# A graph kernel whose grid of source blocks becomes a grid of pairs and eights, with two banks for the sums

## The chip, the cores and the metric

One Trainium2 chip, one of its cores. Times are device microseconds of one execution; a kernel is timed in several runs and the median is given. PE is TensorE, DVE VectorE, ACT ScalarE, POOL GpSimd, SP the queue that issues plain DMAs.

## The reference, cut to what matters

A graph network of 6250 nodes, 206250 edges sorted by destination, 64 features, four layers. In each layer an edge's message is made from its source's features and its own, and a softmax over the edges of a destination, feature by feature, weighs the messages:

```
msg = relu(h[src] + e) + 1e-7
ex = exp(t * msg - segment_max(t * msg, dst))
agg = segment_sum(msg * ex / segment_sum(ex, dst), dst)
out = h + agg
z = relu(layernorm(out @ w1 + b1)) @ w2 + b2      # then h = h + z, and a layernorm
```

`e = edge_attr @ enc_edge_w + enc_edge_b` is the same in all layers. At the start stands a node encoder, at the end a layernorm, a relu and the addition of x.

## The kernel before, in words

Destinations are sorted into 49 blocks of 128, the ones with the most overflow first. Each destination has a row of slots in DRAM (`ecell`), 64 features each, that holds its edges' encoded attributes. The first G slots are a grid: a slot for a group of source blocks. In a slot lies the first edge of this destination whose source is in the group; the nodes of the graph lie in 49 source blocks, of which the first 25 have a slot each and the other 24 share one in pairs, G = 37. Edges that find their slot taken go into overflow slots, V of them in a block (`OVER`, 36 to 6, 613 in sum), S = G + V.

`prepare` runs once. DVE finds for each edge whether an earlier edge of its destination has its cell (`dup`), counts the overflow with a scan (L456), and makes the target row of each edge. POOL scatters the encoded edges to these rows, 128 by an indirect DMA (`encoder`, L289), the first quarter here. Before that 98 DMAs on SP clear `ecell` (L364). DVE goes on with the node encoder (L554 to L582) and with counting rows (L534), for which POOL fetches rows (L526).

`lay` runs once. POOL scatters the other three quarters. Beside it `block` makes, for each destination block, a one-hot table for each source block (`ohd`): DVE reads from the slots which source lies in which slot (`hit`, `pick`, `code`, L798 to L807); PE spreads that number over the partitions (L822, a product with the identity), four slots in a bank; ACT casts it to bf16 (L830); DVE compares it with the partition's number (L837, for a pair twice, L842). SP writes the table of a block, 1568 KB (L847). ACT has the casts and the encoder's copies (L281) in one queue.

`layer` runs four times, three in a loop ("mid") and once more ("last"). For each destination block: SP loads its tables (L922) into one of two buffers; POOL gathers the overflow sources, one indirect DMA a slot (L929), and loads the block's slots from `ecell` (L914). PE (`passes`, L943) multiplies each one-hot table with the source block's features, kept as three bf16 parts, three products a table, eight slots to a bank of PSUM, and for a pair both blocks' into one slot. DVE adds the bank to the slots (`add`, L960) and the gathered rows to the overflow slots (`over`, L970), takes the maximum by halving (`most`, L981, L986), subtracts it (`sub`, L1002); ACT takes the exponent (L1008); DVE multiplies (`mul`, L1016). PE sums over the slots with the identity, four slots of weight and product by a matmul (L1026), and `fold` (L1036) adds the four. After every second block `node_unit` does the layernorms and the two linear maps on DVE, PE and ACT (L1055 to L1160), its steps woven between the operations of the next blocks.

The order is written out in the code and each engine takes its instructions in that order. In block d DVE does: `add` of d (with `passes` of d + 1 on PE, each bank free once it is added), `over`, `most`, `sub` of d, `fold` of d - 1, `mul` of d. PE does: `passes` of d + 1, the node step's products, the sums of d.

## Time and profile before

| | us |
|---|---|
| median of 3 runs | 8189.16 (8177.28 to 8206.0) |
| profiled execution | 8184.75 |
| its span | 8180.6 |
| DVE busy | 5087.6 |
| POOL busy | 5525.4 |
| PE busy | 4289.4 |
| DMA, read and written | 1075 MB |

The page gives the busy time of each engine over the whole span; the stages have different bounds, so the shares of the span say little. A busy PE includes the ends of products, which overlap. An indirect DMA on POOL counts as busy while POOL makes its descriptors. "issue" is a gap in which the engine waited for nothing that the profile shows.

### The profile page before, as it was taken

The numbers are of one execution on the slowest core, as the hardware profiler recorded it, in microseconds if no ns is written. First come the engines' busy times: TensorE is split into PE (matmuls) and PEld (weight loads), VectorE is DVE, ScalarE is ACT, GpSimd is POOL, SyncE is SP. The second block draws the span as 40 slices with busy tenths as digits, with TensorE's granted clock in tenths as the row PEclk, the third lists the DMA queues.
The fourth block names the chain that finished last, engine by engine and source line by source line (L and its number), as shares of the span: only waits on it lengthen the run. The fifth ranks groups of instructions, "written<-read, shape, count | busy, mean of one in ns | idle before, by whom it ended". The sixth has DMA issues, their size and how long they took to land. (4 is left out here: it accounts for less than half of the span.)

```text
span 8180.6 us, 97514 instructions
## 1 busy us (share of the span) xinstructions
PE 4289.4 (52%) x38336; PEld 2718.2 (33%) x38336; DVE 5087.6 (62%) x10507; ACT 1165.7 (14%) x1589; POOL 5525.4 (68%) x4755
## 2 busy tenths in 40 slices
PE   2101122122222137777737787764777773777877
PEld 1100022122121124444424444432444442444444
DVE  8211144333333038889847889884789884777988
ACT  0000012111111001111101111110111110111111
POOL 1676677777676667776537887636877653887874
PEclk5555556555655568888867889886888886788888
DMA  9911122222222144444433444424444443344543
GB/s 417 331 61 31 37 91 95 89 90 80 82 90 89 58 114 144 151 163 160 157 87 129 142 165 161 162 93 130 145 158 155 164 150 87 121 150 139 168 153 101
DMA packets 307868, 1082.09 MB, mean 132 GB/s; under 512 B 147940, under 2 KB 150436, under 8 KB 238276
## 3 DMA queue, kind: packets, MB, share of 16 engines
q0 software_dynamic: 178656, 484.47, 19.7%
q1 hardware_dynamic: 113620, 535.71, 17.6%
q10 hardware_dynamic: 15120, 55.50, 2.2%
q8 instruction: 311, 5.10, 0.3%
q14 instruction: 161, 1.32, 0.0%
HBM read 801.57 MB, written 273.77 MB: 131 GB/s over the span
## 5 line engine op out<-in xcount | busy, mean ns | idle before, releaser
L929 POOL DMA_INDIRECT gb<-ztab,ovi x2452 | 3028.0, 1235 | 874.0 <-issue 738.1
L1026 PE MATMUL bank<-ep_mid,keep 128*128 128x512 f32 (+2 forms) x3750 | 1728.8, 621 | 36.2 <-DVE ep_mid L1016 36.2
L289 POOL DMA_INDIRECT ecell<-es_b,tgi x1212 | 1301.8, 1074 | 496.2 <-issue 364.1
L943 PE MATMUL bank<-zpw,oh_mid 128*128 128x64 bf16 x21609 | 920.3, 203 | 701.0 <-issue 495.8
L943 PEld LDWEIGHTS bank<-zpw,oh_mid 128*128 128x128 bf16 x21609 | 809.4, 104 | 844.7 <-issue 826.2
L1026 PEld LDWEIGHTS bank<-ep_mid,keep 128*128 128x128 f32 x3750 | 760.6, 206 | 970.8 <-issue 890.2
L960 DVE TENSOR_TENSOR xb<-bank,xb 128x512 f32<-128x512 f32 (+1 forms) x980 | 631.4, 646 | 486.7 <-remote 233.9
L822 PE MATMUL bank<-idb,lct 128*128 128x128 bf16 x1813 | 199.1, 281 | 1364.7 <-DVE lct L812 862.6
L822 PEld LDWEIGHTS bank<-idb,lct 128*128 128x128 bf16 x1813 | 160.4, 129 | 1399.3 <-DVE lct L812 871.3
L289 POOL DMA_INDIRECT ecell<-es_a,tgi x400 | 396.7, 992 | 321.4 <-DVE junk L514 174.4
L1026 PE MATMUL bank<-ep_last,keep 128*128 128x512 f32 (+2 forms) x1250 | 578.6, 623 | 13.3 <-DVE ep_last L1016 13.2
L1002 DVE SCALAR_TENSOR_TENSOR ep_mid<-xb,top_x 128x1536 f32<-128x1536 f32 (+10 forms) x303 | 522.0, 1763 | 24.9 <-PE bank L1026 9.8
L1016 DVE SCALAR_TENSOR_TENSOR ep_mid<-xb,ep_mid 128x1536 f32<-128x1536 f32 (+10 forms) x303 | 524.5, 1754 | 0.0
L1157 POOL DMA_INDIRECT ztab<-zb,wri x147 | 184.1, 1252 | 490.0 <-DVE zb L1148 460.1
L1008 ACT ACTIVATE ep_mid<-ep_mid,pack 128x1536 f32<-128x1536 f32 (+10 forms) x303 | 468.0, 1573 | 255.3 <-DVE ep_mid L1002 212.3
L837 DVE TENSOR_SCALAR oh_lay<-cb,keep 128x512 bf16<-128x512 bf16 (+1 forms) x343 | 121.4, 362 | 568.6 <-ACT cb L830 294.9
L981 DVE TENSOR_TENSOR mx<-mx 128x128 f32<-128x128 f32 (+10 forms) x788 | 454.6, 577 | 24.9
L992 ACT ACTIVATE cm<-top_x,nt 128x64 f32<-128x64 f32 x196 | 68.2, 348 | 2802.1 <-DVE top_x L986 2502.1
L943 PE MATMUL bank<-zpw,oh_last 128*128 128x64 bf16 x7203 | 326.1, 205 | 247.4 <-issue 199.8
L914 POOL DMA_INDIRECT xb<-ecell,dci x196 | 239.6, 1223 | 237.2 <-DVE nwf L197 114.3
L830 ACT CAST cb<-bank 128x512 bf16<-128x512 f32 (+1 forms) x490 | 251.5, 569 | 952.3 <-remote 440.6
L943 PEld LDWEIGHTS bank<-zpw,oh_last 128*128 128x128 bf16 x7203 | 281.5, 106 | 302.4 <-issue 296.6
(191 smaller groups left out, 5329.1 us busy)
## 6 DMA issues: line engine op xcount, KB each, us to landing
oh_mid<-ohd SPq DMA_DIRECT2D x147, 1568.0 KB
ecell<-clr SPq DMA_DIRECT2D x98, 1168.0 KB, 30.7
ohd<-oh_lay SPq DMA_DIRECT2D x49, 1568.0 KB
oh_last<-ohd SPq DMA_DIRECT2D x49, 1568.0 KB
gb<-ztab,ovi POOLq DMA_INDIRECT x2452
ea_b<-in_ea ACTq DMA_DIRECT2D x76, 512.0 KB
ecell<-es_b,tgi POOLq DMA_INDIRECT x1212
ea_a<-in_ea ACTq DMA_DIRECT2D x25, 512.0 KB
```

Source lines behind the costliest of these rows:

```text
L289: es_at[b] = es_l[b % 4](GP.indirect_dma_start(T["ecell"], bass.IndirectOffsetOnAxis(ap=tgi[0:n, t % S.TC, t // S.TC:t // S.TC + 1], axis= ...
L822: q = PE.matmul(bank[4 + m % 4][:, 128 * j:128 * j + 128], lct[:, s:s + 1].broadcast_to([128, 128]), idb[:, :], start=True, stop=True)
L830: k_cast[m] = A(AE.copy(cb[:, m % 4, 0:w], bank[4 + m % 4][:, 0:w]))
L914: at["x"][d] = xl_l[d % 2](GP.indirect_dma_start(x_of(d, 0, S.S[d]), None, T["ecell"].rearrange("(n s) f -> n (s f)", s=S.SP), bass.Indire ...
L929: at["g"][d] = ga_l[d % 2](GP.indirect_dma_start(gb[d % 2][:, 64 * v:64 * v + 64], None, T["ztab"], bass.IndirectOffsetOnAxis(ap=ovi[:, i: ...
L943: q = PE.matmul(gps[j % n_gp][:, 64 * (s % 8):64 * (s % 8) + 64], oh[:, d % 2, 128 * b:128 * b + 128], zp[:, b, 64 * part:64 * part + 64], ...
L960: k["add"][d] = V(VE.tensor_tensor(x, gps[j % n_gp][:, 0:64 * (hi - lo)], x, ALU.add))
L981: q = V(VE.tensor_tensor(mx[:, 0:64 * m], src[:, 0:64 * m], src[:, 64 * (n - m):64 * n], ALU.max))
L1002: k["sub"][d, i] = V(VE.scalar_tensor_tensor(ep[:, r, 0:b - a, 64:128], x_of(d, a, b).rearrange("p (s f) -> p s f", f=64), 0.0, top_x[:, d ...
L1008: k["exp"][d, i] = A(AE.activation(ep[:, r, 0:b - a, 0:64], ep[:, r, 0:b - a, 64:128], ACT.Exp, scale=tcol))
L1016: k["mul"][d, i] = k["mul"][d] = V(VE.scalar_tensor_tensor(ep[:, r, 0:b - a, 64:128], x_of(d, a, b).rearrange("p (s f) -> p s f", f=64), 0 ...
L1026: q = PE.matmul(sums[:, 0:w], ident, rows[:, 128 * (c - a):128 * (c - a) + w], start=(c == 0), stop=(c + 4 >= S.S[d]), skip_group_check=True)
```

## The change

The grid gets two steps. The first source block keeps a slot; the other 48 have one slot for each pair (24) and, in a second step, one for each eight blocks (6): G = 31. An edge that finds its pair's slot taken, and is the first such one among its eight, goes into the slot of the eight; only the rest is overflow: `OVER` is now 35 to 3, 516 in sum. S falls from 2426 to 2035 in sum, and the longest row from 73 to 66 slots.

In `prepare` DVE finds the winners for the eights in six rounds of a scan. In `lay` a table of 97 one-hots (1 + 48 + 48) is made instead of 49; for the eights the slot's number is spread in fp32 and compared with eight partition numbers at once by a tensor_tensor. In `layer` the products of a slot run over all its blocks; the tiles for exponents have 24 slots instead of 28; the products have four banks instead of five, and the sums two in turn, so that the sums of block d wait for the fold of d - 2, no longer of d - 1.

```diff
-OVER = (36, 21, 20, 19, 18, 17, 17, 16, 16, 16, 15, 15, 15, 14, 14, 14, 14, 13, 13, 13, 13, 12, 12,
-        12, 12, 12, 11, 11, 11, 11, 11, 10, 10, 10, 10, 10, 9, 9, 9, 9, 8, 8, 8, 7, 7, 7, 6, 6, 6)
+OVER = (35, 20, 18, 17, 17, 16, 15, 15, 14, 14, 13, 13, 13, 12, 12, 12, 12, 11, 11, 11, 11, 10,
+        10, 10, 10, 10, 9, 9, 9, 9, 8, 8, 8, 8, 8, 7, 7, 7, 7, 6, 6, 6, 6, 5, 5, 5, 4, 4, 3)
...
         assert self.ND == len(OVER) == len(EDGES) == 2 * self.pairs - 1
-        singles = 25
-        self.groups = [(b, 1) for b in range(singles)]
-        self.groups += [(b, 2) for b in range(singles, self.ND, 2)]
-        self.singles = singles
+
+
+        self.first = 1 + self.ND // 2
+        self.groups = [(0, 1)] + [(b, 2) for b in range(1, self.ND, 2)]
+        self.groups += [(b, 8) for b in range(1, self.ND, 8)]
         self.G = len(self.groups)
-        assert sum(n for _, n in self.groups) == self.ND
+        self.ones = [sum(n for _, n in self.groups[:s]) for s in range(self.G + 1)]
+        assert self.ND % 8 == 1 and self.G == 31
         self.V = OVER
         self.K = EDGES
...
                 vwait(k)
-                k = V(VE.tensor_scalar(sh2, sh[:, :], float(S.singles), None, ALU.add))
+                k = V(VE.tensor_scalar(sh2, sh[:, :], 1.0, None, ALU.add))
...
                 vwait(k)
+                k_same = k
+                k = V(VE.tensor_scalar(sh[:, 0:N], cell[:, 64:W], 3.0, None, ALU.add))
+                vwait(k)
+                k = V(VE.tensor_scalar(sh[:, 0:N], sh[:, 0:N], 2, None, ALU.logical_shift_right))
+                vwait(k)
+                k_eight = V(VE.tensor_copy(eight, sh[:, 0:N]))
+                k_win = V(VE.memset(win, 0.0))
+                for j in range(S.G - S.first):
+                    vwait(max(k_eight, k_win))
+                    k = V(VE.scalar_tensor_tensor(eq[:, 0, :], eight, j + 1.0, dup[:, :],
+                                                  ALU.is_equal, ALU.mult))
+                    vwait(max(k, k_same))
+                    k = V(VE.tensor_tensor_scan(run[:, 0:N], same[:, :], eq[:, 0, :], 0.0,
+                                                ALU.mult, ALU.add))
+                    vwait(k)
+                    k = V(VE.scalar_tensor_tensor(eq[:, 1, :], run[:, 0:N], 1.0, eq[:, 0, :],
+                                                  ALU.is_equal, ALU.mult))
+                    vwait(k)
+                    k_win = V(VE.tensor_tensor(win, win, eq[:, 1, :], ALU.add))
+                vwait(k_win)
+                V(VE.tensor_tensor(dup[:, :], dup[:, :], win, ALU.subtract))
+                k = V(VE.scalar_tensor_tensor(eight, eight, S.first - 1.0, cell[:, 64:W],
+                                              ALU.add, ALU.subtract))
+                vwait(k)
+                k = V(VE.tensor_tensor(eight, eight, win, ALU.mult))
+                vwait(k)
+                k = V(VE.tensor_tensor(cell[:, 64:W], cell[:, 64:W], eight, ALU.add))
...
             code = sb("code", [128, 80], FP32, yc)
-            lct = sb("lct", [128, G], BF16, yc)
+            lct = sb("lct", [128, S.first], BF16, yc)
+            lcf = sb("lcf", [128, G - S.first], FP32, yc)
+            cbf = sb("cbf", [128, 2, 512], FP32, yc)
             idb = sb("idb", [128, 128], BF16, yc)
             cb = sb("cb", [128, 4, 512], BF16, yc)
-            oh = sb("oh_lay", [128, 2, 128 * ND], BF16, yc)
+            oh = sb("oh_lay", [128, 2, 128 * S.ones[-1]], BF16, yc)
...
             n_four = [0]
-            fours = [list(range(a, min(a + 4, S.singles))) for a in range(0, S.singles, 4)]
-            fours += [list(range(a, min(a + 4, G))) for a in range(S.singles, G, 4)]
+            fours = [[0]] + [list(range(a, min(a + 4, S.first))) for a in range(1, S.first, 4)]
+            fours += [list(range(a, min(a + 4, G))) for a in range(S.first, G, 4)]
...
-                k_lc = V(VE.tensor_tensor(lct[:, :], code[:, 0:G], base, ALU.subtract))
+                V(VE.tensor_tensor(lcf[:, :], code[:, S.first:G], base[:, S.first:G],
+                                   ALU.subtract))
+                k_lc = V(VE.tensor_tensor(lct[:, :], code[:, 0:S.first], base[:, 0:S.first],
+                                          ALU.subtract))
...
                     for j, s in enumerate(four):
+                        if wide < 8:
+                            col, by = lct[:, s:s + 1], idb[:, :]
+                        else:
+                            col, by = lcf[:, s - S.first:s - S.first + 1], ident
                         q = PE.matmul(bank[4 + m % 4][:, 128 * j:128 * j + 128],
-                                      lct[:, s:s + 1].broadcast_to([128, 128]), idb[:, :],
-                                      start=True, stop=True)
+                                      col.broadcast_to([128, 128]), by, start=True, stop=True)
                     k_bc[m] = P(q)
                     AE.wait_ge(pe_s, k_bc[m])
                     if m >= 4:
                         AE.wait_ge(ve_s, k_eq[m - 4])
                     w = 128 * len(four)
-                    k_cast[m] = A(AE.copy(cb[:, m % 4, 0:w], bank[4 + m % 4][:, 0:w]))
+                    spread = cb[:, m % 4, 0:w] if wide < 8 else cbf[:, m % 2, 0:w]
+                    k_cast[m] = A(AE.copy(spread, bank[4 + m % 4][:, 0:w]))
                     VE.wait_ge(ae_s, k_cast[m])
                     if four[0] == 0 and d >= 2:
                         awaits(VE, oh_at[d - 2])
-                    b0, wide = S.groups[four[0]]
-                    to = oh[:, d % 2, 128 * b0:128 * b0 + wide * w]
+                    to = oh[:, d % 2, 128 * S.ones[four[0]]:128 * S.ones[four[-1] + 1]]
                     if wide == 1:
-                        q = V(VE.tensor_scalar(to, cb[:, m % 4, 0:w], prow, None, ALU.is_equal))
+                        q = V(VE.tensor_scalar(to, spread, prow[:, 0:1], None, ALU.is_equal))
+                    elif wide == 2:
+                        to = to.rearrange("p (a t i) -> p a t i", t=2, i=128)
+                        for t in (0, 1):
+                            q = V(VE.tensor_scalar(
+                                to[:, :, t, :], spread.rearrange("p (a i) -> p a i", i=128),
+                                prow[:, t:t + 1], None, ALU.is_equal))
                     else:
-                        to = to.rearrange("p (a t i) -> p a t i", t=2, i=128)
-                        now = cb[:, m % 4, 0:w].rearrange("p (a i) -> p a i", i=128)
-                        for t in (0, 1):
-                            q = V(VE.tensor_scalar(to[:, :, t, :], now, (prow, prow2)[t], None,
-                                                   ALU.is_equal))
+                        for j in range(len(four)):
+                            q = V(VE.tensor_tensor(
+                                to[:, 1024 * j:1024 * j + 1024].rearrange(
+                                    "p (t i) -> p t i", i=128),
+                                spread[:, 128 * j:128 * j + 128][:, None, :].broadcast_to(
+                                    [128, 8, 128]),
+                                prow[:, :, None].broadcast_to([128, 8, 128]), ALU.is_equal))
                     k_eq[m] = q
...
             with lc:
-                n_ep, ep_slots = 3, 28
-                n_gp = 5
+                n_ep, ep_slots = 3, 24
+                n_gp = 4
                 ep = sb("ep_" + tag, [128, n_ep, ep_slots, 128], FP32, lc)
-                oh = sb("oh_" + tag, [128, 2, 128 * ND], BF16, lc)
-                xg = sb("xg_" + tag, [128, 2, 2, 64], FP32, lc) if final else None
-                gps = bank[0:5]
-                sums, NA, NB = bank[5], bank[6], bank[7]
+                oh = sb("oh_" + tag, [128, 2, 128 * S.ones[-1]], BF16, lc)
+                xg = zr if final else None
+                gps = bank[0:4]
+                both, NA, NB = bank[4:6], bank[6], bank[7]
...
                         b0, n = S.groups[s]
                         for b in range(b0, b0 + n):
+                            at_oh = 128 * (S.ones[s] + b - b0)
                             for part in range(3):
                                 q = PE.matmul(
                                     gps[j % n_gp][:, 64 * (s % 8):64 * (s % 8) + 64],
-                                    oh[:, d % 2, 128 * b:128 * b + 128],
...
                     PE.wait_ge(ve_s, k["mul"][d, i])
-                    if i == 0 and d:
-                        PE.wait_ge(ve_s, k["fold"][d - 1])
+                    if i == 0 and d >= 2:
+                        PE.wait_ge(ve_s, k["fold"][d - 2])
                     rows = ep[:, r, :, :].rearrange("p s f -> p (s f)")
                     for c in range(a, b, 4):
                         w = 128 * min(4, b - c)
-                        q = PE.matmul(sums[:, 0:w], ident, rows[:, 128 * (c - a):128 * (c - a) + w],
+                        q = PE.matmul(both[d % 2][:, 0:w], ident, rows[:, 128 * (c - a):128 * (c - a) + w],
                                       start=(c == 0), stop=(c + 4 >= S.S[d]),
                                       skip_group_check=True)
...
                     k["fold"][d] = V(VE.tensor_reduce(
-                        ds[:, u % 2, i, :], sums[:, :].rearrange("p (g c) -> p c g", g=4),
+                        ds[:, u % 2, i, :], both[d % 2][:, :].rearrange("p (g c) -> p c g", g=4),
...
```

Not shown: names and widths of constants, `ohd` with 97 tables, `xg` in the last layer as the tile `zr`.

## Rows read from the trace of the kernel before

**Rows 1.** the page: the span, and busy us of each engine

```profile
span 8180.6 us, 97514 instructions
...
PE 4289.4 (52%) x38336; PEld 2718.2 (33%) x38336; DVE 5087.6 (62%) x10507; ACT 1165.7 (14%) x1589; POOL 5525.4 (68%) x4755
```

**Rows 2.** stretches: length, busy PE, PEld, DVE, ACT, POOL, granted clock, DMA share, GB/s

```profile
961.00:2891.00 1930.00, 411.38 (x3029) 375.63 (x3029) 649.11 (x1128) 329.60 (x642) 1396.99 (x1310) 0.58 0.24 84
...
2891.00:4211.00 1320.00, 927.40 (x8678) 552.19 (x8678) 1042.70 (x2269) 201.27 (x225) 876.91 (x711) 0.83 0.45 142
```

**Rows 3.** timeline of the preparation: start, duration us, engine, line, operation [idle before]

```profile
2.82 291.55 SPq L364 DMA_DIRECT2D ecell<-clr  x98
...
145.00 2.14 DVE L446 TENSOR_TENSOR dup<-dup,eq 128x1728 bf16<-128x1728 bf16 x2
...
154.25 3.76 DVE L456 TENSOR_TENSOR_SCAN run<-same,dup 128x1728 f32<-128x1728 f32 x1
...
158.05 1.96 DVE L461 SCALAR_TENSOR_TENSOR same<-run,cell 128x1728 f32<-128x1728 f32 x1
...
177.24 1.11 POOL L289 DMA_INDIRECT ecell<-es_a,tgi  x1 [174.45 <-DVE junk L514]
...
239.11 0.69 DVE L554 TENSOR_TENSOR zs<-bank,mu 128x512 f32<-128x512 f32 x1 [16.79 <-remote]
...
250.36 1.29 DVE L554 TENSOR_TENSOR zs<-bank,mu 128x512 f32<-128x512 f32 x2 [10.55 <-remote]
...
275.22 0.97 POOL L526 DMA_INDIRECT rw<-in_dch,ni  x1 [32.43 <-DVE junk L534]
```

**Rows 4.** lay stage, groups of 1010 to 2885, one form, two scatters and a L798

```profile
L289 POOL DMA_INDIRECT ecell<-es_b,tgi x1192 | 1277.0, 1071 | 479.8 <-issue 358.3 <-ACT es_b L281 114.9 <-ACT cb L830 6.6
...
L798 DVE TENSOR_TENSOR hit<-i1b,slk 128x1974 bf16<-128x1974 bf16 (+16 forms) x47 | 118.8, 2528 | 0.0
...
L803 DVE TENSOR_TENSOR pick<-hit,srk 128x1974 f32<-128x1974 bf16 (+16 forms) x47 | 118.3, 2518 | 1.6
...
L798 DVE TENSOR_TENSOR hit<-i1b,slk 128x1974 bf16<-128x1974 bf16 x5 | 11.2, 2246 | 0.0
...
1501.48 2.71 DVE L798 TENSOR_TENSOR hit<-i1b,slk 128x2448 bf16<-128x2448 bf16 x1
...
1501.81 3.21 POOL L289 DMA_INDIRECT ecell<-es_b,tgi  x1 [6.68 <-ACT es_b L281]
...
2881.65 0.96 POOL L289 DMA_INDIRECT ecell<-es_b,tgi  x1 [0.30 <-issue]
```

**Rows 5.** groups of 2891:3130, 3130:3510, 3510:4130, and the latter two stretches

```profile
L943 PE MATMUL bank<-zpw,oh_mid 128*128 128x64 bf16 x882 | 41.9, 206 | 157.8 <-DMA oh_mid<-ohd 101.3 <-issue 56.0 <-DVE na L1070 0.5
...
3130.00:3510.00 380.00, 289.77 (x2646) 174.62 (x2645) 320.19 (x661) 62.25 (x66) 303.17 (x244) 0.84 0.46 149
...
L929 POOL DMA_INDIRECT gb<-ztab,ovi x213 | 258.6, 1214 | 64.9 <-issue 63.1 <-DVE cm L1055 0.9 <-DVE na L1076 0.3
...
L943 PE MATMUL bank<-zpw,oh_mid 128*128 128x64 bf16 x2205 | 110.8, 211 | 66.9 <-issue 63.2 <-DVE xb L960 2.1 <-DVE mx L981 0.5
...
L1026 PE MATMUL bank<-ep_mid,keep 128*128 128x512 f32 (+3 forms) x378 | 167.8, 602 | 0.6 <-DVE ep_mid L1016 0.6
...
3510.00:4130.00 620.00, 487.61 (x4835) 291.70 (x4832) 555.63 (x1254) 107.14 (x123) 402.16 (x315) 0.89 0.48 157
...
L943 PE MATMUL bank<-zpw,oh_mid 128*128 128x64 bf16 x4031 | 150.1, 198 | 35.7 <-issue 35.3
...
L1026 PE MATMUL bank<-ep_mid,keep 128*128 128x512 f32 (+3 forms) x678 | 310.8, 618 | 0.0
...
L1079 PE MATMUL bank<-keep,na 128*128 128x128 f32 x14 | 6.5, 462 | 79.1 <-DVE na L1076 79.1
```

**Rows 6.** timeline: products after a slow start of a layer, and a smooth block

```profile
2972.08 8.46 PE L943 MATMUL bank<-zpw,oh_mid 128*128 128x64 bf16 x202 [1.16 <-issue]
...
3638.51 4.45 PE L943 MATMUL bank<-zpw,oh_mid 128*128 128x64 bf16 x147
```

More of the change, by code:

```diff
@@ L131, in scratch @@
     dram("ecell", [S.NN * S.SP, 64])
-    dram("ohd", [S.ND, 128, 128 * S.ND], BF16)
+    dram("ohd", [S.ND, 128, 128 * S.ones[-1]], BF16)
 def build(nc, S, T):
@@ L174, in build @@
         kept = {n: keep[:, a:b] for n, (a, b) in CONST.items() if b <= KEEP_COLS}
[L175 to L176 removed]
+        ident, iota, be, prow, base, full, iota1, we = (
+            kept[n] for n in ("ident", "iota", "be", "prow", "base", "full", "iota1", "we"))
         w1, w2, b1, b2, lng, lnb, g1, bb1, tcol, flip, move = (
@@ L321, in prepare @@
                 sh2 = run[:, :].bitcast(I32)
+                eight, win = key[:, 0, 0:S.CH + 64], key[:, 1, 0:S.CH + 64]
                 xr = zo[:, :, :].rearrange("p j c -> p (j c)")
@@ L1654, in lay_out @@
         "ident": np.eye(128, dtype=f32), "iota": rows(np.arange(128)),
-        "be": rows(p["enc_edge_b"], 2), "prow": part, "prow2": part + 128,
+        "be": rows(p["enc_edge_b"], 2), "prow": part + 128 * np.arange(8, dtype=f32),
         "base": rows([128 * b + 1 for b, _ in S.groups]), "full": rows(S.S),
```

8 lines of the change are left out of this document (4 added, 4 removed).

## The prediction, made before the change was run

> **What bounds the kernel now.** I read the page's totals first, then the busy time by stage, then the groups of each stage. The span is 8180.6 us and no engine is busy for more than 68% of it [rows 1], so each stage has to be read alone. The stages are the preparation (0 to 961), the lay stage (961 to 2891) and four layers: the first, shown, is 1320 us long, the others 1322, 1322 and 1325 [rows 2].
>
> In the preparation the first scatter on POOL starts at 177.24, after a DVE chain that began when the edge lists had landed; the clears keep the DMA engines full until 294 [rows 3].
>
> In the lay stage POOL is the bound: 1192 scatters take 1277 us, the gap of about 0.3 us between two takes another 358, and it waits only 121 us for ACT in 1875 [rows 4]. DVE's work on the one-hot tables (PE, ACT and DVE in turn) lies beside it.
>
> In a layer I take two stretches [rows 5]. From 3130 to 3510 (15 blocks, 2205 one-hot products at 147 a block) POOL is full: 303.2 us busy plus 244 gaps of 0.3 us are 376 of 380. PE is nearly as full: busy 289.8, and of its 90.2 idle 66.9 stand before one-hot products, nearly all put to issue. From 3510 to 4130 (27.4 blocks) DVE is busy 555.6 of 620, PE 487.6; PE's largest wait is 79.1 us for the node step of DVE (L1079). So a block takes 25.3 us in the first and 22.6 in the second stretch, and three engines stand within some 10% of each other. That is the point on which the case turns: the change takes load off POOL and DVE and puts it on PE.
>
> **The change part by part.**
>
> *Preparation.* Six rounds of a scan and three elementwise operations over 1728 elements come ahead of the scan L456 in DVE's chain. Prices [rows 3]: the scan 3.76 us, a scalar_tensor_tensor 1.96 (L461), a bf16 tensor_tensor 1.07 (L446). A round is 3.76 + 2 x 1.96 + 1.07 = 8.75, six are 52.5; the eight operations around them (two integer steps, copy, memset, subtract, scalar_tensor_tensor, product, sum) I price at six x 1.07 + 2 x 1.96 = 10.3. POOL's first scatter comes 63 us later. Part comes back. DVE now waits 16.8 and 10.6 us at L554 for products that stand on PE behind edge tiles, which load against full DMA engines, and POOL then waits 32.4 us for DVE (L534) [rows 3]. The clears shrink with the cell rows from 73 to 66 slots and end near 266, and this stretch moves from 222 to 285, behind them. So 27 of the 63 are regained: +36. Bounds: +31 (all of POOL's wait goes) and +63.
>
> *Lay stage, the tables.* Of a block's 13 tensor_scalar comparisons 13 stay (1 for the single, 12 for pairs), and 6 tensor_tensor comparisons of 1024 fp32 elements come, 294 in all. The nearest row is L798, 2246 ns for 1974 elements, 1.14 ns each: 1.17 us, 344 us of DVE. DVE has the room (about a third busy [rows 2]). What matters is POOL. An undisturbed scatter takes 0.96 us; one issued when the tensor_tensor L798 has just begun took 3.21; the mean of the stage is 1071 ns [rows 4]. The excess, 0.113 x 1192 = 135 us, comes with 237 us of L798 and L803, both tensor_tensor on two SBUF tiles: 0.57 us of POOL for each us of such work. So 344 x 0.57 = 196 us more, less 16% of the 135 (slots times edges fall from 114387 to 96203, 21 us): +175. Bounds: 0, if these comparisons disturb nothing, and +344, if POOL stands still under all of them. The doubled table writes (1568 to 3104 KB a block) have room: DMA share 0.24 [rows 2].
>
> The Trainium skill, SBUF — State Buffer, section "Who interferes with whom", says that a tensor_tensor takes only the read side of the port that VectorE shares with GpSimd, and infers that it leaves GpSimd's making of descriptors alone. By that the sum would have 0 here instead of 175. The trace speaks against it [rows 4].
>
> *Layers, POOL.* The overflow slots go from 613 to 516, 97 gathers fewer in a layer at 1.21 + 0.30 us: 147 us of POOL, but only the first 20 blocks or so wait for POOL, and they lose 42 gathers: at most 64 us.
>
> *Layers, DVE.* A block has 41.5 slots instead of 49.5 on average. The two elementwise passes save 2 x 511 elements, the maxima 478, the two additions 511 and one instruction: at about 1.05 ns an element 2.2 us a block, 57 in the later stretch.
>
> *Layers, PE.* A slot of a pair or of eight needs its blocks' one-hot products summed: 1 + 48 + 48 = 97 tables of 3 products instead of 49, that is 291 instead of 147 a block. The smooth price is 4.45 us for 147 [rows 6], 30.3 ns each at the full clock. The matrix sums (L1026) fall from 625 to 527 a layer. Early stretch: 144 x 15 products at 30 to 50 ns (110.8 us for 2205 [rows 5]); at the clock of 0.84 I take 37.5, +81; sums -26; so 289.8 + 81 - 26 = 345 busy. The issue gaps of 67 stay in the main, and 12 of the other waits: 424 against 380. As POOL is then no longer full (some 320 of 424), I let a part of the gaps go: +30. Later stretch: +120 (full clock), sums -49: 559 busy, with 36 of gaps, 17 of waits at L1085 and L1103 and some of L1079's left, 620: 0. Head of a layer: the first tables land some 5 us later, but the first block is held until about 2972 by slow issue [rows 5, 6], beside the gathers: 0. Together +30 a layer, +120. Bounds: -120, if PE takes it all (64 + 57 above), and +130, if the gaps grow with the products (67 and 36 doubled, on top of +30).
>
> *Two banks for the sums, four for the products.* The fold of block d - 1 stands ahead of the first product pass of block d on DVE, and the sums wait for that pass, so the wait for the fold never ends last; the little wait of L1026 is for L1016 [rows 5]. Four groups of slots on four banks repeat five on five. Both 0; if DVE's order were another, the cover would be a 0.7 us fold a block, 34 a layer. Smaller tiles (24 slots) keep 101 slices a layer: 0. The tables double to 3104 KB a block; with two buffers a load has more than a block's time: 0, and if it were late it would be at most its own landing of some 10 us in a few blocks.
>
> *Sum.* The profiled execution took 8184.75 us, 4.15 beyond its span, and the median is 8189.16. 8184.75 + 36 + 175 + 120 = 8516; 4 more for the median: 8520.
>
> **The rivals.**
>
> *Gathers and DVE were the bound (faster).* PE hides the new products in its waits (90 us early, 132 later) and the layer ends by POOL and DVE. For it: POOL at 376 of 380. Against it: PE's waits there are issue gaps inside the same products. Price -121 a layer, -484; with +211 ahead of the layers 7916. It decides from a layer that is 53 us shorter; half way, at -75 a layer, 8100. Chance 0.16.
>
> *The added comparisons leave POOL alone, and PE just absorbs its products.* Then 8189 + 36 + (0 to 60), 8200 to 8290. For it: L798 runs long and the new ones are short. Chance 0.20. The Trainium skill's rule above belongs here.
>
> *The issue gaps grow with the products.* 56 us of such gaps stand in the head of a layer, 67 early, 36 later [rows 5]; if they belong to the instructions rather than to the state of POOL, layers take +130 each: 8189 + 211 + 520 = 8920. Against it: a run of 147 went without any [rows 6]. Chance 0.14.
>
> **How the numbers follow.** My forecast, PE slightly over its room and POOL disturbed in the lay stage, has 0.50 and 8300 to 8750 as its own range. About 0.3% (25 us) is what a measurement of this kernel can tell from no change. Faster by more is the first rival but for its edge: 0.15. Within it: 0.06, from the second rival's low end and between. Slower: 0.79. As cases of both signs hold chance, the range of 8 in 10 is 8150 to 8880: it leaves out the far end of the first rival and of the third.
>
> **What would show it.** First scatter at 240 instead of 177; POOL's mean scatter in the lay stage near 1.2 us instead of 1.07; L943's successor with 57036 products and in the early blocks PE busy above 85% with POOL waiting for DVE; DVE at 80 to 85% in late blocks with waits for PE at the fold. Wrong would be: layers under 1270 us (PE was not the bound), layers over 1400 (gaps grew), or scatters that keep 1.07 us.

## The result, and the profile after

The changed kernel takes 9004.35 us (median of 4, 8989.88 to 9009.84) against 8193.29 us (4 runs beside it): ratio 1.0988, 95% interval 1.0964 to 1.1012. 8520 was forecast, with 8880 as the upper end. The sign was right and the loss was two and a half times as large, 811 us for 331.

Where the 820.2 us of span went, by the start of the first `cm` exponential of each layer (3058.2, 4564.3, 6065.6, 7573.6 after; 2984.8, 4305.9, 5627.5, 6950.2 before): 73.4 ahead of the first of them, then 185.0, 180.2, 185.3 in three layers and 196.3 in the last with its tail. So the layers have nine tenths of it. (`cm` is the exponential of a block's maximum, which ACT takes once a block.) From the page, with the groups that answer to [rows 1, 4]:

```profile
span 9000.8 us, 152034 instructions
PE 5006.3 (56%) x65776; PEld 3589.3 (40%) x65776; DVE 4968.2 (55%) x10686; ACT 1050.8 (12%) x1540; POOL 4861.2 (54%) x4367
...
L976 POOL DMA_INDIRECT gb<-ztab,ovi x2064 | 2302.9, 1116 | 1055.0 <-issue 603.8
L991 PE MATMUL bank<-zpw,oh_mid 128*128 128x64 bf16 x42777 | 1758.5, 203 | 1005.7 <-issue 816.6
L291 POOL DMA_INDIRECT ecell<-es_b,tgi x1212 | 1384.1, 1142 | 415.8 <-issue 369.8
...
L991 PE MATMUL bank<-zpw,oh_last 128*128 128x64 bf16 x14259 | 612.0, 205 | 338.5 <-issue 293.1
L1155 DVE TENSOR_TENSOR h<-h,bank 128x128 f32<-128x128 f32 x100 | 28.7, 287 | 1388.9 <-PE bank L1151 1388.9
...
L885 DVE TENSOR_TENSOR oh_lay<-cbf,keep 128x1024 bf16<-128x1024 f32 x294 | 340.0, 1220 | 270.6 <-issue 191.0
```

No engine has filled up. PE idles 1344 us before its products (L991, both groups), mostly put to issue, and DVE 1389 us at one instruction, the h addition L1155 (336 us in the trace of before, there L1107), for the linear2 products on PE. The stages, in the columns of [rows 2]:

```profile
0.00:1040.00 1040.00, 121.68 (x611) 105.03 (x611) 366.43 (x470) 39.79 (x74) 556.73 (x558) 0.54 0.42 158
1040.00:2965.00 1925.00, 418.67 (x3013) 396.83 (x3013) 902.08 (x1463) 299.05 (x591) 1485.45 (x1306) 0.60 0.33 123
2965.00:4475.00 1510.00, 1111.38 (x15538) 765.85 (x15538) 929.26 (x2221) 179.95 (x225) 690.72 (x617) 0.82 0.47 166
```

From block 3 on the odd blocks have this form, their pass shrinking along the layer (30.7 us in block 5, 23.1 in block 17, 15.2 in block 33, 8.7 in block 47, in which no gather falls). Shown are stretches before, in and behind the pass over the products of block 11 in the first layer, the pass once more cut in three where the granted clock changes, and then its timeline:

```profile
3360.00:3382.00 22.00, 19.52 (x307) 13.36 (x304) 19.39 (x50) 4.10 (x5) 6.58 (x6) 1.00 0.56 221
3382.00:3396.40 14.40, 12.97 (x53) 6.73 (x53) 13.31 (x33) 0.27 (x1) 11.35 (x11) 0.88 0.65 244
3396.40:3424.50 28.10, 14.95 (x295) 12.79 (x292) 6.40 (x8) 3.18 (x3) 15.64 (x15) 0.64 0.27 70
3424.50:3440.00 15.50, 14.84 (x187) 9.26 (x186) 13.32 (x41) 1.18 (x3) 1.86 (x2) 1.00 0.74 300
...
3396.40:3400.80 4.40, 2.07 (x52) 1.69 (x49) 4.19 (x7) 1.77 (x2) 3.49 (x4) 1.00 0.51 105
3400.80:3421.30 20.50, 9.67 (x138) 7.91 (x139) 2.21 (x2) 1.41 (x2) 12.15 (x12) 0.50 0.26 73
3421.30:3424.50 3.20, 3.20 (x109) 3.19 (x106) 0.00 (x0) 0.00 (x0) 0.00 (x0) 1.00 0.02 5
```
```profile
3396.35 1.24 PE L991 MATMUL bank<-zpw,oh_mid 128*128 128x64 bf16 x37
3398.03 0.28 PE L991 MATMUL bank<-zpw,oh_mid 128*128 128x64 bf16 x4 [0.43 <-issue]
3399.46 0.28 PE L991 MATMUL bank<-zpw,oh_mid 128*128 128x64 bf16 x4 [1.15 <-issue]
3400.19 0.32 PE L991 MATMUL bank<-zpw,oh_mid 128*128 128x64 bf16 x5 [0.45 <-issue]
...
3412.62 0.34 PE L991 MATMUL bank<-zpw,oh_mid 128*128 128x64 bf16 x3 [1.04 <-issue]
3412.86 0.94 POOL L976 DMA_INDIRECT gb<-ztab,ovi  x1 [0.30 <-issue]
3414.04 0.37 PE L991 MATMUL bank<-zpw,oh_mid 128*128 128x64 bf16 x4 [1.09 <-issue]
3414.11 0.94 POOL L976 DMA_INDIRECT gb<-ztab,ovi  x1 [0.30 <-issue]
3415.36 0.94 POOL L976 DMA_INDIRECT gb<-ztab,ovi  x1 [0.30 <-issue]
3416.18 0.37 PE L991 MATMUL bank<-zpw,oh_mid 128*128 128x64 bf16 x4 [1.77 <-issue]
3418.30 6.18 PE L991 MATMUL bank<-zpw,oh_mid 128*128 128x64 bf16 x160 [1.74 <-issue]
3424.31 0.42 PE L1144 MATMUL bank<-keep,hb 128*128 128x128 f32 x2
...
3426.08 0.29 DVE L1155 TENSOR_TENSOR h<-h,bank 128x128 f32<-128x128 f32 x1 [23.07 <-PE bank L1151]
```

While POOL issues gathers one behind another, the products come three or four at a time with a microsecond or more between (over the whole pass mostly three to six, with 0.2 to 1.8 us); the last gather starts at 3415.36, and from 3418.30 on 160 products run in 6.18 us. The pass takes 28 us at a mean granted clock of 0.64, though PE ran at 1.00 from 3360 to 3382 and does so again behind the pass. Inside it the gaps come first: three of them, 0.43, 1.15 and 0.45 us, stand ahead of 3400.8, where the clock is still 1.00 (its level of 2.4 GHz); then it is 0.50 (1.2 GHz) until 3421.3, 3 us after the products have begun to run without gaps. DVE waits 23.07 us meanwhile, since the transposes (L1144) for linear2 stand behind the whole pass in PE's order.

I added up, for each layer, the time from the first to the last product of every block's pass ("pass time") and the idle time inside ("gaps"). First layer: 462 us with 157 of gaps before, 861 with 276 after. So a pass product costs 42 ns without its gaps before (305 us for 7203) and 41 after (586 for 14259), not the 30 to 37.5 of the forecast, and the gaps grew by 119. In after_2, below, the same working gives 30.5 ns (435 us for 14259) at 25 us of gaps: the 41 ns go with the gaps and the lower clock beside them.

### The profile page after: what moved, and what is told of

Read it like the earlier page. It is cut to its first block and busy times, and to the rows that moved or that the text cites. A ratio compares the mean times of both kernels' runs of the same rounds, so it can differ in the third digit from the quotient of the medians.

```text
span 9000.8 us, 152034 instructions
## 1 busy us (share of the span) xinstructions
PE 5006.3 (56%) x65776; PEld 3589.3 (40%) x65776; DVE 4968.2 (55%) x10686; ACT 1050.8 (12%) x1540; POOL 4861.2 (54%) x4367
## 2 busy tenths in 40 slices
DMA packets 295662, 1395.68 MB, mean 155 GB/s; under 512 B 141732, under 2 KB 144228, under 8 KB 225860
## 5 line engine op out<-in xcount | busy, mean ns | idle before, releaser
L976 POOL DMA_INDIRECT gb<-ztab,ovi x2064 | 2302.9, 1116 | 1055.0 <-issue 603.8
L991 PE MATMUL bank<-zpw,oh_mid 128*128 128x64 bf16 x42777 | 1758.5, 203 | 1005.7 <-issue 816.6
L991 PEld LDWEIGHTS bank<-zpw,oh_mid 128*128 128x128 bf16 x42777 | 1569.5, 105 | 1227.3 <-issue 1204.1
L291 POOL DMA_INDIRECT ecell<-es_b,tgi x1212 | 1384.1, 1142 | 415.8 <-issue 369.8
L1074 PE MATMUL bank<-ep_mid,keep 128*128 128x512 f32 (+1 forms) x3162 | 1449.4, 617 | 12.7 <-DVE ep_mid L1064 12.6
L991 PE MATMUL bank<-zpw,oh_last 128*128 128x64 bf16 x14259 | 612.0, 205 | 338.5 <-issue 293.1
L1155 DVE TENSOR_TENSOR h<-h,bank 128x128 f32<-128x128 f32 x100 | 28.7, 287 | 1388.9 <-PE bank L1151 1388.9
L991 PEld LDWEIGHTS bank<-zpw,oh_last 128*128 128x128 bf16 x14259 | 542.6, 106 | 419.1 <-issue 413.7
L885 DVE TENSOR_TENSOR oh_lay<-cbf,keep 128x1024 bf16<-128x1024 f32 x294 | 340.0, 1220 | 270.6 <-issue 191.0
L1074 PE MATMUL bank<-ep_last,keep 128*128 128x512 f32 (+3 forms) x1054 | 475.3, 609 | 4.7 <-DVE ep_last L1064 4.7
L1050 DVE SCALAR_TENSOR_TENSOR ep_mid<-xb,top_x 128x1280 f32<-128x1280 f32 (+12 forms) x303 | 445.7, 1511 | 22.4 <-PE bank L1074 5.0
L1064 DVE SCALAR_TENSOR_TENSOR ep_mid<-xb,ep_mid 128x1280 f32<-128x1280 f32 (+12 forms) x303 | 445.4, 1491 | 0.0
L1056 ACT ACTIVATE ep_mid<-ep_mid,pack 128x1280 f32<-128x1280 f32 (+12 forms) x303 | 403.6, 1366 | 214.2 <-DVE ep_mid L1050 181.6
L1029 DVE TENSOR_TENSOR mx<-mx 128x192 f32<-128x192 f32 (+10 forms) x788 | 405.6, 515 | 20.3
```

The costliest lines, as they stand in the source:

```text
L291: es_at[b] = es_l[b % 4](GP.indirect_dma_start(T["ecell"], bass.IndirectOffsetOnAxis(ap=tgi[0:n, t % S.TC, t // S.TC:t // S.TC + 1], axis= ...
L885: q = V(VE.tensor_tensor(to[:, 1024 * j:1024 * j + 1024].rearrange("p (t i) -> p t i", i=128), spread[:, 128 * j:128 * j + 128][:, None, : ...
L976: at["g"][d] = ga_l[d % 2](GP.indirect_dma_start(gb[d % 2][:, 64 * v:64 * v + 64], None, T["ztab"], bass.IndirectOffsetOnAxis(ap=ovi[:, i: ...
L991: q = PE.matmul(gps[j % n_gp][:, 64 * (s % 8):64 * (s % 8) + 64], oh[:, d % 2, at_oh:at_oh + 128], zp[:, b, 64 * part:64 * part + 64], sta ...
L1029: q = V(VE.tensor_tensor(mx[:, 0:64 * m], src[:, 0:64 * m], src[:, 64 * (n - m):64 * n], ALU.max))
L1050: k["sub"][d, i] = V(VE.scalar_tensor_tensor(ep[:, r, 0:b - a, 64:128], x_of(d, a, b).rearrange("p (s f) -> p s f", f=64), 0.0, top_x[:, d ...
```

## The experiments

My theory was that the products cost their time in the chain, through DVE's wait for linear2; the rival was that they cost it by slow issue, which needs the gathers. The first set of runs brought a third thing to light: the same kernel has different speeds in different sets of runs (a set is the runs timed together, with the kernel before among them). In some the kernel before takes 7769 to 7773 us, in others 8193 to 8380. I call them quick and slow sets; the result above is from a slow one.

What differs is not known: the expectations below speak of chips, but the record gives chip 15 both for the first, quick set and for a slow one a quarter of an hour later (0 is quick, 8 and 11 are slow), so it can be a condition of a chip as well as the chip. The slow sets differ by 2% among themselves. The kind also shows in each run's own trace, ahead of the layers: in the versions of the kernel after, the lay stage's first scatter starts at 974 to 977 us in quick sets and at 1029 to 1037 in slow ones. Each kernel is compared with its neighbours in sets of the same kind. Layer lengths are those from one layer's first `cm` to the next.

| kernel | quick: us; layer; gaps a layer | slow: us; layer; gaps a layer |
|---|---|---|
| before | 7773, 7769 | 8193, 8372, 8377, 8380; 1321 to 1370; 157 to 203 |
| after | 7517; 1159 to 1169; 12 to 25 | 9004, 9205; 1501 to 1539; 273 to 324 |
| before_products | 7962, 7952; 1307 to 1312; 10 to 16 | 9509; 1635 to 1650; 305 to 325 |
| few_products | 7336; 1108 to 1117; 0 to 7 | 8435; 1357 to 1363; 194 to 247 |
| one_gather | 7268, 7266; 1100 to 1106; 4 to 5 | 7290; 1077 to 1079; 26 to 29 |
| plain_loads | | 7402; 1105 to 1112; 12 to 15 |
| late_h | 7381, 7392; 1109 to 1132; 19 to 33 | 9523; 1603 to 1612; 301 to 419 |
| before_late_h | | 8230; 1317 to 1320; 178 to 246 |
| one_bank | | 9189; 1530 to 1541; 285 to 320 |
| scalar_eights | | 9186; 1534 to 1543; 290 to 320 |

**The kernels unchanged.** after_again and before_again ran in a slow set, after_2 in a quick one.

> The kernel after, unchanged, on the chip that these runs get, since the four experiments so far ran on a chip on which the kernel before takes 7773 us and on which products follow one another almost without gaps (14 to 28 us of gaps a layer inside the passes, against 275 in the trace of the kernel after). Theory 1 (the 811 us are the slow issue of products, which the trace of before already had at 157 to 203 us a layer): on a chip of that kind the kernel after has gaps under 50 us a layer, layers of 1150 to 1250, and takes 7500 to 7850, about as long as the kernel before or less. Theory 2 (the order of the node step on PE costs the time whatever the issue does): layers stay above 1400 and the kernel at 8500 or more. On a chip with slow issue: 9000 again.

> The kernel before, unchanged, for its trace beside the others of this chip. On a chip where it takes 7773 us the 410 us less than in the first trace should be found in the layers, as gaps inside the passes (157 to 203 us a layer in the first trace) that are gone; the preparation and the lay stage within 30 us of the first trace. If the two chips differ otherwise (clock of PE, DMA), the difference is spread over all stages.

> The kernel after, unchanged, beside the three others. With slow issue 9000 to 9250 us. With quick issue, theory 1 (the 811 us are slow issue): layers of 1130 to 1200 and 7450 to 7700 in all, faster than the kernel before there (7773); theory 2 (the node step's place on PE costs the time whatever the issue does): layers above 1400.

after_again: 9204.62 against 8372.24, ratio 1.0999 (1.0957 to 1.104), the first result once more. after_2: 7517.44 once against 7769.41 (7 runs), 0.968, with no interval. So **the change is slower by 10% in slow sets and about 3% faster in a quick one**, the latter from one run. before_again fell in a slow set, so the kernel before has no trace from a quick one. Its layers there can be bounded: before_products_2 has its first `cm` at 2793, and 7770 - 2793 leaves 4977 us for the layers where after_2 has 7513 - 2936 = 4577. That is 100 us a layer in favour of the change. One layer each of after_again (slow) and after_2 (quick), same columns:

```profile
3088.00:4619.00 1531.00, 1119.38 (x15538) 769.81 (x15536) 929.11 (x2222) 180.35 (x226) 691.26 (x615) 0.81 0.46 162
```
```profile
2936.00:4102.00 1166.00, 960.37 (x15538) 669.33 (x15538) 928.63 (x2220) 179.58 (x225) 694.54 (x613) 0.92 0.61 216
```

DVE, ACT and POOL have the same work to within 4 us; only PE's differs, by its clock, and the length. The groups of after_2 behind 2940 show PE with hardly any issue gaps, and the wait of the h addition at 307 us:

```profile
L991 PE MATMUL bank<-zpw,oh_mid 128*128 128x64 bf16 x42195 | 1277.3, 194 | 155.2 <-DMA oh_mid<-ohd 89.6 <-issue 40.3 <-DVE nwf L208 14.4
...
L1155 DVE TENSOR_TENSOR h<-h,bank 128x128 f32<-128x128 f32 x100 | 28.7, 287 | 307.0 <-PE bank L1151 307.0
```

**before_products: only the products, twice.**

```diff
-                        for b in range(b0, b0 + n):
+                        for b in [*range(b0, b0 + n)] * 2:
```

> The kernel before with every product of the passes issued twice (294 a block instead of 147; the second set replaces the first, so nothing else changes: 613 gathers, 49.5 slots, one bank for the sums, tables of 1568 KB). Theory 1 (products in the chain, and slow to be issued beside gathers): layers rise from 1322 to 1520 or more, 8980 or more in all. Theory 2 (the account of the prediction by engine totals): early blocks +80 to +95 a layer, later blocks hide 120 us in PE's waits of 132: layers 1400 to 1420, 8500 to 8580 in all.

> The kernel before with every product issued twice. With quick issue the layers are 1307 to 1312. If this run meets slow issue: theory 1 (gaps grow with the number of products) gaps of 300 us or more a layer inside the passes and layers of 1520 to 1650; theory 2 (a fixed stretch of slow issue a block) gaps near 180 us, layers 1400 to 1450.

The first ran in a quick set: 7962.47 against 7772.57, 190 us for 4 x 7203 added products, 6.6 ns each. That is 47 us a layer, where the account by engine totals had 80 to 95 and theory 1 200: neither has the number, and theory 1 is far off. The second ran in a slow set: layers of 1643 on average against 1358 of before_again, 285 us for 7203 products, 40 ns each, and gaps of 305 to 325 against 168 to 189. Theory 1 of the second expectation holds: gaps go with the number of products. Products alone, with nothing else of the change, make the layers of a slow set longer than those of the changed kernel.

**few_products: 126 of the 291 products left out.**

```diff
-                        for b in range(b0, b0 + n):
+                        for b in range(b0, b0 + (n if n < 8 else 1)):
```

> The kernel after with one table of eight in the passes of the slots for eight (165 products a block instead of 291; what these slots add is wrong, all else stays). Theory 1 (the pass over the products stands whole in the chain of every second block, since linear2 of the node step waits behind it on PE and DVE waits for linear2): layers fall from 1510 to between 1260 and 1330, DVE's wait ahead of the h addition from 1389 us to under 500. Theory 2 (the products are not what lengthens the layers; smaller slots, other banks or the doubled table loads are): layers stay above 1450.

> The kernel after with 165 products a block instead of 291 (one table of eight in the passes of the slots for eight). With quick issue it takes 7336, layers of 1108 to 1117. If this run meets slow issue: theory 1 (the time goes with the number of products that come slowly) gaps of 150 to 200 us a layer as in the kernel before, and layers of 1250 to 1330; theory 2 (something else of the change lengthens the layers there) layers above 1450.

In the quick set the layers are 1113 against 1165 of after_2, 8 ns a product; in the slow one 1359 against 1534 of after_again, 28 ns. The quick layers are 150 us under what I expected, for I had reckoned from the trace of the kernel after. Those of few_products_3 are 30 us over, and its gaps (194 to 247) reach over the 200 expected. DVE there still waits 1082 us for linear2, so that wait does not go away with the products that caused the loss. With 165 products a block instead of 147, and with 97 gathers fewer, its layers are as long as those of before_again (1358): in a slow set the smaller grid by itself buys little.

**one_gather and plain_loads: what makes the issue slow.** In one_gather a block has a single overflow gather. In plain_loads every gather is a DMA of the same size that SP issues, and SP takes over the wait ahead of them (the data are others).

```diff
-                        at["g"][d] = ga_l[d % 2](GP.indirect_dma_start(
-                            gb[d % 2][:, 64 * v:64 * v + 64], None, T["ztab"],
-                            bass.IndirectOffsetOnAxis(ap=ovi[:, i:i + 1], axis=0)))
+                        at["g"][d] = ga_l[d % 2](SP.dma_start(
+                            gb[d % 2][:, 64 * v:64 * v + 64],
+                            table[128 * v:128 * v + 128, 0:64]))
```

> The kernel after with one overflow gather a block instead of 10.5 on average (the rest of the gathered tile is zero; the output lacks those edges). Theory 1 (PE gets its products slowly while POOL issues gathers back to back): the idle time inside the passes falls from about 275 us a layer to under 80, passes of 28 us go, layers fall from 1510 to between 1250 and 1350. Theory 2 (the gaps belong to the number of products and have nothing to do with the gathers): gaps stay above 200 us a layer and layers above 1450, for POOL was not the bound.

> The kernel after with one overflow gather a block. With quick issue it takes 7264 to 7268 and shows 4 us of gaps inside the passes a layer. If this run meets slow issue: theory 1 (the products come slowly because POOL's gathers run) gaps under 80 us a layer, layers 1100 to 1200, some 7500 in all; theory 2 (the supply of instructions is slow there by itself) gaps above 200 us, layers above 1400, 8900 or more.

> The kernel after with each of its 2064 overflow gathers replaced by a plain DMA of the same size (128 rows of 256 bytes of the same table) that SP issues; the rows are the wrong ones. POOL then makes no descriptors for them, but as many packets go into the same buffer. If this run meets slow issue: theory 1 (POOL's making and queueing of gathers slows the supply of products) gaps under 50 us a layer inside the passes and layers of 1080 to 1200, as with one gather; theory 2 (the small packets in the DMA engines do it, whoever issues them) gaps above 200 us and layers above 1400. With quick issue it tells only what the gathers cost by themselves: 7260 to 7520.

one_gather takes 7267.94 in a quick set and 7290.29 in a slow one, where the kernel before takes 8377: without the gathers the two kinds are alike in the layers (1100 to 1106 and 1077 to 1079). plain_loads takes 7401.78 in a slow set (before 8380.14), with as many bytes as the kernel after (1395.77 MB in all against 1395.68) in many more and smaller packets (526841 against 295662). Its layer:

```profile
3056.00:4168.00 1112.00, 945.16 (x15538) 658.70 (x15538) 924.76 (x2221) 180.07 (x226) 116.25 (x98) 0.94 0.61 224
```

Clock 0.94 instead of 0.81, gaps 12 to 15 us a layer. So it is shown that the slow issue comes with POOL's own gathers; the same bytes in more and smaller packets do not bring it. plain_loads changes three things at once, though: who issues, by which queue, and that the rows are read in order instead of at random. Which of them counts was not tested apart. Slower fetching of PE's instructions is not seen: the packets of the instruction queue take 1.07 us on average in the layers of after_again and 1.08 in those of after_2. Theory 1 holds in all three; the layers of one_gather came out 20 us (slow) and 150 us (quick) below the lower end I gave.

**late_h and before_late_h: the h addition later.** The edit takes no step of the node unit between the products of DVE (`mul`) of the block in which linear2 is issued, so that the h addition comes behind the additions of the next block.

```diff
-                        if not ready or i == n - 1:
+                        if ready and i == n - 1:
                             steps(4, "normed")
```

> The kernel after with the h addition of the node step and what follows it taken behind the adds of the next block instead of between two mul slices of the same block. Theory 1 (DVE's wait for linear2 is the extra time): that wait falls from 1389 us to under 500 and the layers from 1510 to between 1380 and 1430, the whole to about 8600. Theory 2 (PE is full: whatever DVE does not wait for here it waits for at the next add): layers stay within 30 us of 1510, and the wait moves to the add of the products.

> late_h on the chip that these runs get. If it meets slow issue: theory 1 (the slow pass costs through DVE's wait for linear2) layers 1400 to 1450 against 1501 to 1532 of the kernel after, 8600 to 8750 in all; theory 2 (the slow pass is the period itself) layers 1480 or more. With quick issue: 7380 to 7395, 0.953 of the kernel before.

> The kernel before with the h addition of the node step taken behind the adds of the next block, as in late_h. Theory 1 (DVE's wait for linear2, 336 us at L1107 in the first trace, can be had): 150 to 300 us faster than before. Theory 2 (POOL is the bound of the early blocks, PE and DVE of the late ones, and this wait only moves): within 60 us of before.

Quick sets: 7381.16 against 7772.57, ratio 0.951 (0.9487 to 0.9533), and a second time 0.9529 (0.9505 to 0.9553), some 130 us less than after_2; DVE's wait at L1155 is 116 us there. Slow set: 9523.06 against 8377.46, 1.1376 (1.1334 to 1.1419), worse than the kernel after by 320 us. The layers (1603 to 1612) are in the range of theory 2, but neither theory had them longer than those of the kernel after. Its groups behind 3090:

```profile
L1205 POOL DMA_INDIRECT ztab<-zb,wri x147 | 226.4, 1540 | 1509.6 <-DVE zb L1196 1487.7 <-issue 21.9
...
L1136 DVE TENSOR_TENSOR hb<-bank,pack 128x256 f32<-128x256 f32 x100 | 42.4, 424 | 1198.9 <-PE bank L1133 1180.5 <-issue 18.4
L1155 DVE TENSOR_TENSOR h<-h,bank 128x128 f32<-128x128 f32 x100 | 28.7, 287 | 1136.7 <-PE bank L1151 1136.7
```

In after_again the same three waits are 775.0, 558.4 and 1393.8. The wait at L1155 shrank by 257 us, that for linear1 (L1136) grew by 640, and POOL now stands 1510 us at the z rows with the gathers behind them. So **my theory falls** in the form I gave it: with the h addition out of the way, DVE waits for PE at another step of the node unit instead. DVE's wait for linear2 is where the slow pass shows; that it is what makes it cost time is not borne out. What exactly makes late_h worse than the kernel after there stays open. On the kernel before the same edit helps in a slow set: 8229.66 against 8372.24, 0.9829 (0.9791 to 0.9867). That is 143 us, just under the 150 that I gave as the least; DVE's wait at L1107 falls from 530 to 274 us.

**scalar_eights: the tensor_tensor comparisons of the lay stage as tensor_scalar.**

```diff
-                        for j in range(len(four)):
-                            q = V(VE.tensor_tensor(
...
+                        for t in range(8):
+                            q = V(VE.tensor_scalar(
+                                to[:, :, t, :], spread.rearrange("p (a i) -> p a i", i=128),
+                                prow[:, t:t + 1], None, ALU.is_equal))
```

> The kernel after with the comparisons for the slots of eight in the lay stage as 16 tensor_scalar instructions of 512 or 256 elements a block in place of 6 tensor_tensor of 1024. Theory 1 (tensor_tensor on two SBUF inputs slows POOL's scatters): the mean of the lay stage's scatter falls from 1142 ns to 1060 to 1090, about 80 us of POOL. Theory 2 (any long DVE work does, or none): it stays within 20 ns of the kernel after. The lay stage is 0 to 80 us shorter, since POOL's waits may take it back.

Theory 1 holds: the mean scatter is 1069 ns, about what it was before the change (1071, [rows 4]), for 1135 in after_again in the same set.

```profile
L291 POOL DMA_INDIRECT ecell<-es_b,tgi x1212 | 1295.3, 1069 | 523.6 <-issue 362.1
...
L886 DVE TENSOR_SCALAR oh_lay<-cbf,keep 128x256 bf16<-128x256 f32 (+1 forms) x784 | 278.6, 428 | 359.8 <-issue 262.1
```

Of the 80 us of POOL, 21 reach the stage (from the first to the last of these scatters 1929.6 us, 1950.2 in after_again), the rest is waits for ACT. The whole is the same, 9186 for 9205. The new comparisons are shorter as well as of another form, but the trace of the kernel after tells the two apart:

```profile
1504.77 2.30 DVE L839 TENSOR_REDUCE code<-pick 128x43 f32<-128x2064 f32 x1
1505.87 0.96 POOL L291 DMA_INDIRECT ecell<-es_b,tgi  x1 [0.30 <-issue]
...
1523.31 6.90 DVE L885 TENSOR_TENSOR oh_lay<-cbf,keep 128x1024 bf16<-128x1024 f32 x6 [4.34 <-issue]
...
1525.67 1.97 POOL L291 DMA_INDIRECT ecell<-es_b,tgi  x1 [0.30 <-issue]
```

Under a reduction of 2.30 us with one input a scatter keeps its 0.96 us; under the tensor_tensor instructions of 1.2 us it takes 1.97. So it is the form and not the length. The tensor_scalar comparisons are not quite free: scatters that run beside them alone take 1.09 us on average (182 of them in scalar_eights), against 1.48 beside the tensor_tensor form (172 in after_again).

**one_bank: one bank for the sums, as before.**

```diff
-                    if i == 0 and d >= 2:
-                        PE.wait_ge(ve_s, k["fold"][d - 2])
+                    if i == 0 and d:
+                        PE.wait_ge(ve_s, k["fold"][d - 1])
```

> The kernel after with the matrix sums of all blocks in one bank, so that a block's sums wait for the fold of the block before, as in the kernel before. By the prediction (the fold stands ahead of the products of the next block on DVE) the two banks bring nothing: 0.9675 of before with quick issue, 1.10 with slow issue, each within 0.005. By the rival (PE could run a block's sums ahead of the fold) it is 0.7 us a block slower or more, 140 us in all, 0.985 or 1.117.

9189.22 against 8380.14, 1.0978 (1.0944 to 1.1012): the two banks bring nothing, as forecast.

Two more runs, one_gather_2 and before_products_2, repeated their kernels in a second quick set within 11 us.

## Why the prediction was wrong

*Layers, +120 forecast, about +747 measured in the slow set.* This is the step that failed: "The issue gaps of 67 stay in the main" and "Later stretch: ... 620: 0". Two sizes in it were off. The product was priced at 37.5 and 30.3 ns, from the one smooth block [rows 6], while the average of all passes in the first layer, gaps left out, was 42 ns: +280 us of PE a layer where I had 201 for 42 of its 49 blocks. And the gaps were kept as they were; they grew by 119 a layer, 1.75 times for 1.98 times the products. PE's passes grew by 399 a layer, 98 sums less give back some 60 (0.6 us each), and PE's waits could take only part of the rest: 185 a layer. Both sizes have one source: where the gaps are gone a product costs 30.5 ns (after_2), which is the price that I had. With the gaps the clock falls, as shown above for block 11 (0.50 from behind the third gap until the products ran without any), and it is 0.81 over a slow layer against 0.92 over a quick one. A smaller slip, which changes nothing: the first 20 blocks lose 35 gathers, not 42, so that "at most 64 us" is 53.

*The third rival was the right one here.* It had "layers take +130 each", 8920 and a chance of 0.14, and the sign "layers over 1400 (gaps grew)" came true at 1501 to 1508. That its 8920 lies within 85 us of the result is in part luck: the layers took 747 us and not 520, and what stands ahead of them 73 and not 211. My argument against it, "a run of 147 went without any" [rows 6], was weak: the passes run without gaps where POOL issues no gathers in a row, as from 3418.30 on above. So it was with that very run of 147, which starts at 3638.51: POOL's last gather before it starts at 3635.70 and the next at 3644.12. one_gather and plain_loads show that this is the condition.

*The first rival was right in the quick sets.* There PE does take the products in its waits and the layers shrink by about 100 us (bounded above), for its -121: fewer gathers and fewer slots pay. So the forecast's own mechanism, PE slightly over its room, is what neither kind of set shows. It mixed the traits of both: prices from a stretch without gaps, and a bound from one with them.

*Preparation, +36 forecast.* The first scatter came at 238.28 (240 forecast), so the rounds were priced right. But nothing of it was regained; the lay stage's first scatter moved from 974.0 to 1033.8, by 60. In the slow set the waits of [rows 3] stand nearly unchanged (17.5 and 7.1 us for 16.8 and 10.6, and 32.5 for 32.4), although the clears now end at 247 and the DMA engines are busy for 11% of the time from 285 to 304:

```profile
189.53 57.62 SPq L367 DMA_DIRECT2D ecell<-clr  x20
...
238.28 1.11 POOL L291 DMA_INDIRECT ecell<-es_a,tgi  x1 [235.68 <-DVE junk L544]
```
```profile
303.68 0.69 DVE L584 TENSOR_TENSOR zs<-bank,mu 128x512 f32<-128x512 f32 x1 [17.48 <-issue]
...
336.28 0.98 POOL L556 DMA_INDIRECT rw<-in_dch,ni  x1 [32.45 <-DVE junk L564]
```

So full DMA engines were not their cause. By the code these products stand on PE behind edge tiles whose ACT copies wait until POOL has scattered an earlier tile of 16, and POOL's pace did not change; this was not tested.

*Lay stage, +175 forecast.* The stretch of the es_b scatters grew by 14 us (1908.9 to 1922.6) in the first pair of traces, by 34 in the second (1916.5 to 1950.2), and by 83 in quick sets (before_products_2 1803.8, after_2 1887.2). DVE's part was right, 340 us for 344. The disturbance is real but smaller: 82 us of scatters (1301.8 to 1384.1) for 340 us of comparisons, 0.24, or 0.30 with the 21 us added that the shorter rows save, for the 0.57 that I took from two long instructions of another form. In the slow set POOL's waits for ACT ahead of the scatters then gave most of it back (125.5 us before, 39.7 after); in quick sets they are under 7 us (before_products_2 and after_2). The Trainium skill, SBUF — State Buffer, section "Who interferes with whom", infers that a tensor_tensor leaves descriptor making alone. scalar_eights contradicts it for this form, 1135 ns against 1069 with the tensor_scalar form of the same comparisons, and the measurement decides.

*Two banks, 0.* Right by one_bank, which differs from after_again by less than 0.2% (9189 and 9205, in different slow sets). Four product banks and 24-slot tiles were not tried apart; the doubled tables cost nothing that stands out beyond the head of a layer, where PE waits for them (89.6 us in three layers of after_2).

## What to carry to other kernels

Before pricing instructions onto an engine, see whether those it already has are issued smoothly, and beside what: an added product cost 6 to 8 ns of time in a quick set and 28 to 40 in a slow one, beside POOL's gathers. A large and named issue gap in the trace of before is a term of the sum, and it grows with the instructions put beside it. A wait shown at one instruction may only be where a slow engine becomes visible; moving the instruction moved the wait. And a change that trades gathers for products should be timed in more than one set of runs, with the old kernel in each: here its sign depends on the set.

## What the runs showed of the hardware

- Two kinds of sets of runs: the kernel before takes 7769 to 7773 us in one and 8193 to 8380 in the other, and in the layers the difference is the idle time inside runs of products and the lower clock that goes with it (after: 12 to 25 us of gaps a layer against 273 to 324). Outside the layers the slow kind is longer too: the lay stage's first scatter comes at 974 instead of 914 in before_products, though the very first comes at 177 on both. What makes a set slow, no trace tells, and chip 15 has both.
- The slow issue goes with POOL's gathers, one behind another. With one gather a block the gaps are 26 to 29 us a layer in a slow set, and with the same bytes issued by SP 12 to 15 (7402 us against 9205 in all).
- POOL's gathers themselves are not slower in the slow kind: 1116 ns (after) against 1127 (after_2).
- TensorE's granted clock fell from 1.00 to 0.50 in a pass behind three gaps of 0.4 to 1.2 us, and rose again 3 us after the products ran without gaps (block 11 of the kernel after).
- A tensor_tensor of 1024 elements with two inputs in SBUF lengthens POOL's indirect DMAs (1.97 us under a row of them for 0.96); the tensor_scalar form lengthens them less (1135 and 1069 ns on average over the stage), and a reduction of 2.30 us with one input not at all (0.96).
- Of the versions tried, with all gathers and products in place, late_h is the fastest in a quick set (0.951) and the slowest in a slow one (1.138); before_late_h is the only one that was faster than before in a slow set (0.983), and it was not run in a quick one. One that beats both kernels on both kinds was not found.
